# A scan layer and its router: dot products on TensorE, statistics spread, products in place

## The chip, the cores and the metric

The kernel runs on one core of a Trainium2 chip. The metric is the device time of one execution in microseconds; three executions of the kernel before gave 4455.1, 4456.08 and 4457.46 us, so the median is 4456.08 us. A core has five engines that run their own instruction streams and wait for each other by semaphores: TensorE (PE in the profile), VectorE (DVE), ScalarE (ACT), GpSimd (POOL) and SyncE (SP), which here starts all the DMAs of the part in question.

## What is computed

Two layers. The first is a selective state space layer on 16 batches of 1024 rows of 512 numbers, the second a layer that lets only some rows through attention and an MLP, chosen by a router's score. Cut to what matters:

```python
xh = _layernorm(x)                                 # 16 x 1024 x 512
xp = einsum('bld,ed->ble', xh, x_proj_w)           # 64 for the rank, 16 B, 16 C
delta = softplus(einsum('blr,dr->bld', xp[..., :64], dt_proj_w) + dt_proj_b)
h = exp(delta * A) * h + delta * B * xh            # step by step over the 1024 rows
y = (h * C).sum(n) + xh * D                        # 16 states n
x1 = x + y
hn = _layernorm(x1)
weights = (hn @ router_w)[..., 0] + router_b[0]    # one score a row
# top_k of the scores picks rows; those go through attention and an MLP
out = x1 + (result for chosen rows, hn for the others)
```

## The kernel before

`scan_phase` is the first part. It runs over 16 batches; a loop body holds two of them (lines 829 and following on VectorE). A batch has 16 chunks of 32 channels, and a chunk has 4 groups g of 4 states, so that a tile (c, g) is 128 partitions (4 states x 32 channels) by 1024 rows. For each tile:

- ScalarE makes the decay exp(delta A) into one of three PSUM places (`exp_decay`, line 671), and once a chunk copies delta times x there (`copy_dx`, 677).
- VectorE multiplies that by B into `inp` (`make_input`, 810). For the fourth group (`OWN`) of the chunks in `OWN_AT`, 1 to 13, GpSimd does it from SBUF (917).
- VectorE runs the recurrence, one scan instruction, into `hid[:, g]` (821). It waits for `ch_ready` of the same group one chunk earlier, that is until GpSimd has read the old states.
- GpSimd multiplies `hid` by C into `ch` (955).
- TensorE sums the states into `ps_y` (`sum_states`, 444, behind the skip term, 439), ScalarE copies `ps_y` to `ysb` (`copy_y`, 684), TensorE turns it and adds x (`turn_y`, 455 and 456), and ScalarE writes x1 back into `xr` (`copy_x1`, 691).

Every engine's program is written out in order by hand. Beside a chunk's tiles stands work for the batch before and the batch after, put at a pair (c, g) or (c, place) by tables at the top of the file: in chunks 0 to 2 ScalarE takes the second statistics of the batch before (`SUMS2`, 17 steps: 8 sums, a mean, 8 sums of squares), in chunks 3 and 4 it makes the output rows (`MAKE_OUT`), in chunks 5 and 6 the first statistics of the next batch (`SUMS1`), in 7 to 10 it normalises and copies the transposes made by TensorE (`TURN`, `COPY_XHAT`), in 10 and 11 the projections (`PROJECT`, `COPY_PROJ`, 404 and 545), and from 12 on delta (`Z`, `LOG`, 415, 563 to 581). GpSimd does ten steps of 128 x 1024 for delta (`DELTA`), small Newton series for both statistics (`FINISH1`, `FINISH2`, 878 to 887) and the end of the router (`route`, 906 and 909). `aux` is one PSUM bank which all these side jobs of TensorE pass through one after the other, in the order of `USES`.

The router before: ScalarE copies `router_w` into `aux` (`copy_rw`, 590), and VectorE takes eight dot products of 128 rows by 512 channels (`router`, 834), four after the scans of chunk 2 and four after those of chunk 3, each with the mean as its scalar. `make_out` overwrites the rows and waits for them. After the last batch the same work stands alone: `copy_rw`, the 17 steps, the router, Newton, `route`, a transpose of all the scores (505), and their DMA; behind that VectorE picks rows by the scores.

`ffn_phase`, with attention and MLP, follows at about 3475 us and is not touched.

## Time and profile before

| | |
|---|---|
| median of 3 executions | 4456.08 us |
| profiled execution | 4463.26 us |
| its span, first to last instruction | 4461.5 us |
| mean granted TensorE clock | 0.756 |
| VectorE busy | 3768.9 us (84%) |
| GpSimd busy | 3363.5 us (75%) |
| TensorE busy (matmul) | 3066.8 us (69%) |
| ScalarE busy | 2861.0 us (64%) |

The profile is of one execution. Busy shares are means over the whole span with its two phases. A timeline row gives the start in us from the span's start, the time of one instruction or of a run of equal ones (x4), the engine, the line, what is written and read, and in brackets the idle time before it and what ended it. Matmuls of float32 stand in the profile as two instructions each, with two weight loads.

### The profile page before, as it was taken

The numbers are of one execution on the slowest core, as the hardware profiler recorded it, in microseconds if no ns is written. First come the engines' busy times: TensorE is split into PE (matmuls) and PEld (weight loads), VectorE is DVE, ScalarE is ACT, GpSimd is POOL, SyncE is SP. The second block draws the span as 40 slices with busy tenths as digits, with TensorE's granted clock in tenths as the row PEclk, the third lists the DMA queues.
The fourth block names the chain that finished last, engine by engine and source line by source line (L and its number), as shares of the span: only waits on it lengthen the run. The fifth ranks groups of instructions, "written<-read, shape, count | busy, mean of one in ns | idle before, by whom it ended". The sixth has DMA issues, their size and how long they took to land. (4 is left out here: it accounts for less than half of the span.)

```text
span 4461.5 us, 61468 instructions
## 1 busy us (share of the span) xinstructions
PE 3066.8 (69%) x17574; PEld 1408.3 (32%) x17574; DVE 3768.9 (84%) x3027; ACT 2861.0 (64%) x4425; POOL 3363.5 (75%) x1716
## 2 busy tenths in 40 slices
PE   4667665766676666665665756666664289999997
PEld 1222232322232222222232323222222145555553
DVE  2999999999999999999999999999998754555552
ACT  5777777777778687868777777777774223332221
POOL 3999999999999999999999999999998100000010
PEclk7767676767766676667676767676775589999998
DMA  4454546463646455554545464636453300000000
GB/s 102 104 136 121 148 114 158 96 170 87 171 101 156 114 144 130 127 136 122 134 123 135 124 152 105 164 84 180 92 146 76 144 22 20 19 19 19 19 19 8
DMA packets 198219, 472.94 MB, mean 106 GB/s; under 512 B 60688, under 2 KB 61200, under 8 KB 197088
## 3 DMA queue, kind: packets, MB, share of 16 engines
q1 hardware_dynamic: 177136, 452.11, 40.3%
q0 software_dynamic: 20736, 16.88, 1.4%
q8 instruction: 135, 2.21, 0.2%
...
## 5 line engine op out<-in xcount | busy, mean ns | idle before, releaser
L955 POOL TENSOR_TENSOR ch<-hid,cmat 128x1024 f32<-128x1024 f32 x1024 | 2385.4, 2358 | 92.7 <-DVE hid L821 76.4
L821 DVE TENSOR_TENSOR_SCAN hid<-place,inp 128x1024 f32<-128x1024 f32 x1024 | 2266.1, 2270 | 105.4 <-ACT place L671 87.3
L671 ACT ACTIVATE place<-delr,a_neg 128x1024 f32<-128x1024 f32 x1024 | 1126.8, 1111 | 293.6 <-DVE hid L821 190.2
L444 PE MATMUL ps_y<-ch,nsum 128*32 128x256 f32 x8192 | 856.5, 517 | 424.3 <-POOL ch L955 423.4
L810 DVE TENSOR_TENSOR inp<-place,bmat 128x1024 f32<-128x1024 f32 x816 | 941.6, 1211 | 64.2 <-ACT place L677 63.4
L455 PE MATMUL ps_y<-ident,ysb 128*128 128x128 f32 x1024 | 319.2, 408 | 599.0 <-ACT ysb L684 580.0
L444 PEld LDWEIGHTS ps_y<-ch,nsum 128*32 128x32 f32 x8192 | 254.6, 137 | 1025.6 <-POOL ch L955 753.2
L917 POOL TENSOR_TENSOR inp<-dxr,bmat 128x1024 f32<-128x1024 f32 x208 | 490.2, 2357 | 0.0
L455 PEld LDWEIGHTS ps_y<-ident,ysb 128*128 128x128 f32 x1024 | 230.5, 278 | 807.9 <-ACT ysb L684 759.1
...
L439 PE MATMUL ps_y<-xhT,dskip 128*32 128x256 f32 x2048 | 260.8, 600 | 134.2 <-ACT xr L691 134.2
L677 ACT ACTIVATE place<-dxr 128x1024 f32<-128x1024 f32 x256 | 261.7, 1022 | 95.9 <-DVE hid L821 92.9
L456 PE MATMUL ps_y<-xr,ident 128*128 128x128 f32 x1024 | 286.6, 377 | 0.0
L456 PEld LDWEIGHTS ps_y<-xr,ident 128*128 128x128 f32 x1024 | 241.0, 289 | 0.0
L415 PE MATMUL aux<-xpT,dtw 64*128 64x512 f32 x256 | 218.2, 946 | 21.3 <-ACT dxT L564 20.5
L1282 PE MATMUL ps_t<-w,h2T 128*128 128x512 f32 x512 | 226.2, 600 | 0.7 <-ACT h2T L1423 0.7
L691 ACT ACTIVATE xr<-ps_y 128x256 f32<-128x256 f32 x256 | 97.6, 381 | 195.0 <-PE ps_y L456 194.3
L1306 PE MATMUL ps_m<-w,gT 128*128 128x512 f32 x512 | 222.4, 592 | 0.0
L1182 POOL COPY idx_x<-cols_i 128x1 uint32 (+1 forms) x16 | 3.0, 185 | 250.7 <-DMA out_rows<-row,idx_out 175.7
L609 ACT ACTIVATE squares<-xr,m 128x512 bf16<-128x512 f32 x256 | 181.2, 710 | 0.6
L1699 DVE COPY msel<-ps_m 128x128 f32<-128x128 f32 x16 | 4.7, 292 | 208.9 <-PE ps_m L1351 208.0
L684 ACT ACTIVATE ysb<-ps_y 128x256 f32<-128x256 f32 x256 | 94.0, 367 | 120.1 <-PE ps_y L444 120.1
...
## 6 DMA issues: line engine op xcount, KB each, us to landing
dxr<-dxT SPq DMA_DIRECT2D x1024, 128.0 KB, 2.4
delr<-delT SPq DMA_DIRECT2D x1024, 128.0 KB, 2.4
...
bmat<-b_and_c SPq DMA_DIRECT2D x256, 128.0 KB, 3.4
cmat<-b_and_c SPq DMA_DIRECT2D x256, 128.0 KB, 3.1
...
```

The lines of the kernel that those rows point to most:

```text
L439: pe.matmul(ps_y[q * CH:(q + 1) * CH, 0:2 * P], dskip[:, k, c % NT * CH:(c % NT + 1) * CH], xhT[:, i, j, q * 2 * P:(q + 1) * 2 * P], start ...
L444: last = pe.matmul(ps_y[q * CH:(q + 1) * CH, 0:2 * P], nsum[:], ch[:, g, q * 2 * P:(q + 1) * 2 * P], start=False, stop=(g == GROUPS - 1))
L455: pe.matmul(out_t, ysb[:, t * P:(t + 1) * P], ident[:], start=True, stop=False)
L456: last = pe.matmul(out_t.rearrange("p (q d) -> p q d", q=4), ident[:], x_t, start=False, stop=True)
L671: nc.scalar.activation(place[:, PLACE[par, c, g], :], delr[:, c % 2, :], ACT.Exp, scale=a_neg[:, i:i + 1])\
L677: nc.scalar.activation(place[:, PLACE[par, c, "dx"], :], dxr[:, c % 2, :], ACT.Copy).then_inc(dx_ready, 1)
L810: nc.vector.tensor_tensor(inp[:, g, :], place[:, PLACE[par, c, "dx"], :], bmat[:, g, :], ALU.mult).then_inc(inp_ready, 1)
L821: nc.vector.tensor_tensor_scan(hid[:, g, :], place[:, PLACE[par, c, g], :], inp[:, g, :], 0.0, ALU.mult, ALU.add).then_inc(hid_ready, 1)
L917: nc.gpsimd.tensor_tensor(inp[:, OWN, :], dxr[:, c % 2, :], bmat[:, OWN, :], ALU.mult)\
L955: nc.gpsimd.tensor_tensor(ch[:, g, :], hid[:, g, :], cmat[:, g, :], ALU.mult).then_inc(ch_ready, 1)
L1282: last = pe.matmul(one[bank], xT[:, k, :], w(k), start=(k == 0), stop=(k == n - 1))
L1306: last = pe.matmul(one["m1"], gT[:, k, :], w_2[:, k, :], start=(k == 0), stop=(k == F // P - 1))
```

## The change

Three things, all in `scan_phase`.

1. The router's scores come from TensorE. A row's dot product of x1 with `router_w` is split in two. The x part: `w_xproj` gets 32 more columns that all hold `router_w`, so that the projection of the normalised rows yields a further line block of `xpT`; `router_x` brings it into rows by 8 matmuls of one column, `copy_router_x` copies them, and `scale_route_x` on GpSimd undoes the normalisation (times the standard deviation, plus mean times the sum of `router_w`). The y part: `ysb` keeps all 16 chunks of a batch, and `router_y` multiplies each chunk (two blocks of 128 rows as weights) with 4 columns of `rw_chunk`, in five pieces (`ROUTE_Y`) during chunks 0 and 1 of the next batch. `copy_router_y` copies the result, and `route` on GpSimd puts the parts together, with 5 instructions in place of 2. VectorE's `router` and ScalarE's `copy_rw` go. The first `ADD_TERMS` entries move from chunks 0 and 1 to 1 to 3, and a delta step from chunk 2 to 3. For the last batch the five pieces stand at the end, in front of the statistics.
2. `SUMS1` begins at (5, 0) with one step for each place, and waits for each half of the rows by itself.
3. GpSimd writes its product with C over `hid`; `ch` goes. A scan now waits for `ch_summed`, TensorE's sum, of the same group one chunk earlier.

Besides, `OWN_AT` becomes chunks 2 to 12, so that VectorE makes two more input products a batch and GpSimd two fewer.

```diff
--- before.py
+++ after.py
-SUMS1 = {(5, 3): range(0, 3), (6, 0): range(3, 6), (6, 1): range(6, 9), (6, 2): range(9, 13), (6, 3): range(13, 17)}
+SUMS1 = {(5, 0): range(0, 1), (5, 1): range(1, 2), (5, 2): range(2, 3), (5, 3): range(3, 5), (6, 0): range(5, 7),
+         (6, 1): range(7, 10), (6, 2): range(10, 13), (6, 3): range(13, 17)}
...
-         (2, 3): (0, 2, 3), (7, 3): (0, 3, 3)}
-
-
-ADD_TERMS = {(2, 0): ((0, 2), (0, 3), (1, 1)), (2, 1): ((1, 1), (1, 2), (2, 1)),
+         (3, 1): (0, 2, 3), (7, 3): (0, 3, 3)}
...
-ADD_TERMS = {(2, 0): ((0, 2), (0, 3), (1, 1)), (2, 1): ((1, 1), (1, 2), (2, 1)),
+         (3, 1): (0, 2, 3), (7, 3): (0, 3, 3)}
+
+
+ADD_TERMS = {(2, 0): ((1, 3), (1, 3), (2, 1)), (2, 1): ((2, 1), (2, 2), (3, 0)),
...
-RW_COPY = (2, 1)
-ROUTER = (2, 3)
+ROUTE_Y = {(0, 1): range(0, 4), (0, 2): range(4, 6), (0, 3): range(6, 11), (1, 1): range(11, 14), (1, 2): range(14, 16)}
+COPY_ROUTE_Y = (2, 0)
+ROUTE_X = (14, 0)
+COPY_ROUTE_X = (14, 3)
+SCALE_ROUTE_X = (15, 1)
+ROUTE_READ = {cs[0]: i + 1 for i, cs in enumerate(ROUTE_Y.values())}
...
-OWN_AT = tuple(range(1, 14))
+OWN_AT = tuple(range(2, 13))
...
-        xproj = sb("xproj", [P, KD, R + 2 * N])
+        xproj = sb("xproj", [P, KD, P])
...
-        ch = sb("ch", [P, GROUPS, L])
-        ysb = sb("ysb", [P, 2 * P])
+        ysb = sb("ysb", [P, CHUNKS, 2 * P])
...
-                    last = pe.matmul(aux[0:R + 2 * N, :], xproj[:, k, :],
+                    last = pe.matmul(aux[:], xproj[:, k, :],
...
-                if k == 3 and h == 0 and has(b, 1):
-                    pe.wait_ge(router_sum, b * TC)
...
+            def router_x(b):
+
+                aux_free(b, ("route_x",))
+                for t in range(TC):
+                    last = pe.matmul(aux[:, t:t + 1], xpT[R + 2 * N:P, t * P:(t + 1) * P],
+                                     ident[R + 2 * N:P, R + 2 * N:R + 2 * N + 1], start=True, stop=True)
+                last.then_inc(aux_full, 1)
+
+            def router_y(b, cs, emptied):
+
+                if 0 in cs:
+                    pe.wait_ge(aux_emptied, emptied)
+                for c in cs:
+                    for t in range(2):
+                        last = pe.matmul(aux[:, 4 * t:4 * t + 4], ysb[:, c, t * P:(t + 1) * P], rw_chunk[:, c, :],
+                                         start=(c == 0 and t == 0), stop=(c == CHUNKS - 1 and t == 1))
+                last.then_inc(route_y_full, 1)
...
+                    if (k, h) == (2, 0) and has(b, 1):
+                        pe.wait_ge(route_y_copied, b)
...
-                                     ch[:, g, q * 2 * P:(q + 1) * 2 * P],
+                                     hid[:, g, q * 2 * P:(q + 1) * 2 * P],
...
+                        if (c, g) in ROUTE_Y and has(b, 1):
+                            router_y(b - 1, ROUTE_Y[c, g], b * NUSE + USE["z", 2, 1] + 1)
+                        if (c, g) == ROUTE_X and not final:
+                            router_x(b + 1)
...
+            for cs in ROUTE_Y.values():
+                router_y(nb_run - 1, cs, nb_run * NUSE)
...
-            def copy_rw(b, emptied):
-
-                act.wait_ge(aux_emptied, emptied)
-                nc.scalar.activation(aux[:], rw[:], ACT.Copy).then_inc(rw_ready, 1)
+            def copy_router_x(b):
+
+                if has(b, 1):
+                    act.wait_ge(route_in_step, b * 3)
+                aux_filled(b, ("route_x",))
+                nc.scalar.activation(route_x[:], aux[:, 0:TC], ACT.Copy).then_inc(aux_emptied, 1)
+
+            def copy_router_y(b):
+
+                if has(b, 1):
+                    act.wait_ge(wcol_ready, b)
+                act.wait_ge(route_y_full, b * len(ROUTE_Y) + len(ROUTE_Y))
+                nc.scalar.activation(route_y[:].rearrange("p (q t) -> p t q", t=2),
+                                     aux[:, 0:TC].rearrange("p (t q) -> p t q", t=2), ACT.Copy)\
+                    .then_inc(route_y_copied, 1)
...
+                for h in range(2):
+                    if 4 * h in steps:
+                        act.wait_ge(x_in[par][h], (b - par) * 8 + 16)
...
-                    act.wait_ge(ln2, b * LN2 + LN2 - 1)
-
-                    act.wait_ge(router_sum, b * TC + t + 4)
+                    act.wait_ge(ln2, b * LN2 + LN2)
...
-                nc.scalar.activation(ysb[:], ps_y[:, 0:2 * P], ACT.Copy).then_inc(ysb_ready, 1)
+                if c in ROUTE_READ and has(b, 1):
+                    act.wait_ge(route_y_full, (b - 1) * len(ROUTE_Y) + ROUTE_READ[c])
+                nc.scalar.activation(ysb[:, c, :], ps_y[:, 0:2 * P], ACT.Copy).then_inc(ysb_ready, 1)
...
-            copy_rw(last, nb_run * NUSE)
+            copy_router_y(last)
...
-                    dve.wait_ge(ch_ready, tile(b, c, g) - GROUPS + 1)
+                    dve.wait_ge(ch_summed, tile(b, c, g) - GROUPS + 1)
...
-            def router(b, par, h):
-
-                if h == 0:
-                    dve.wait_ge(rw_ready, b + 1)
-                    if has(b, 1):
-                        dve.wait_ge(wcol_ready, b)
-                    dve.wait_ge(ln2_act, b * LN_ACT + 9)
-                for t in range(4 * h, 4 * h + 4):
-                    if has(b, 1) or t > 0:
-                        dve.wait_ge(router_sum, b * TC + t)
-                    nc.vector.scalar_tensor_tensor(junk[:], xr[:, par, t, :], m2[:, 1, t:t + 1], aux[:],
-                                                   ALU.add, ALU.mult, accum_out=r2[:, 8, t:t + 1])\
-                        .then_inc(router_sum, 1)
...
-            last = nb_run - 1
-            for h in range(2):
-                router(last, 1, h)
...
+                nc.gpsimd.tensor_tensor(r1[:, 7, :], r1[:, 0, :], r1[:, 4, :], ALU.mult).then_inc(ln1, 1)
...
-            def route(b):
-
-                pool.wait_ge(router_sum, b * TC + TC)
-                nc.gpsimd.tensor_tensor(r2[:, 3, :], r2[:, 8, :], r2[:, 4, :], ALU.mult).then_inc(ln2, 1)
+            def scale_route_x(b, par):
+
+                n = b * 3
+                pool.wait_ge(aux_emptied, b * NUSE + USE["route_x",] + 1)
+                pool.wait_ge(ln1, b * LN1 + LN1)
+                if has(b, 2):
+                    pool.wait_ge(route_step, (b - 1) * ROUTE_STEPS)
+                nc.gpsimd.tensor_tensor(route_in[:, par, 1, :], m1[:, 1, :], rw_sum[:].to_broadcast([P, TC]), ALU.mult)\
+                    .then_inc(route_in_step, 1)
+                nc.gpsimd.tensor_tensor(route_in[:, par, 0, :], route_x[:], r1[:, 7, :], ALU.mult)\
+                    .then_inc(route_in_step, 1)
+                pool.wait_ge(route_in_step, n + 2)
+                nc.gpsimd.tensor_tensor(route_in[:, par, 0, :], route_in[:, par, 0, :], route_in[:, par, 1, :],
+                                        ALU.subtract).then_inc(route_in_step, 1)
+
+            def route(b, par):
+
+                n = b * ROUTE_STEPS
                 pool.wait_ge(ln2, b * LN2 + LN2)
+                pool.wait_ge(route_y_copied, b + 1)
+                pool.wait_ge(route_in_step, b * 3 + 3)
+                if has(b, 1):
+                    pool.wait_ge(wcol_ready, b)
+                nc.gpsimd.tensor_tensor(route_t[:, 0, :], m2[:, 1, :], rw_sum[:].to_broadcast([P, TC]), ALU.mult)\
+                    .then_inc(route_step, 1)
+                nc.gpsimd.tensor_tensor(route_t[:, 1, :], route_y[:], route_in[:, par, 0, :], ALU.add)\
+                    .then_inc(route_step, 1)
+                pool.wait_ge(route_step, n + 2)
+                nc.gpsimd.tensor_tensor(route_t[:, 2, :], route_t[:, 1, :], route_t[:, 0, :], ALU.add)\
+                    .then_inc(route_step, 1)
+                pool.wait_ge(route_step, n + 3)
+                nc.gpsimd.tensor_tensor(route_t[:, 1, :], route_t[:, 2, :], r2[:, 4, :], ALU.mult)\
+                    .then_inc(route_step, 1)
+                pool.wait_ge(route_step, n + 4)
                 pool.sem_inc(refining, 1)
-                nc.gpsimd.tensor_tensor(wcol[:, bass.ds(b * TC, TC)], r2[:, 3, :], rb[:].to_broadcast([P, TC]),
+                nc.gpsimd.tensor_tensor(wcol[:, bass.ds(b * TC, TC)], route_t[:, 1, :], rb[:].to_broadcast([P, TC]),
...
-                            pool.wait_ge(ch_summed, tile(b, c, g) - GROUPS + 1)
-                        nc.gpsimd.tensor_tensor(ch[:, g, :], hid[:, g, :], cmat[:, g, :],
+                        nc.gpsimd.tensor_tensor(hid[:, g, :], hid[:, g, :], cmat[:, g, :],
...
+                        if (c, g) == SCALE_ROUTE_X and not final:
+                            scale_route_x(b + 1, 1 - par)
...
-        "w_xproj": rows(i["L0_attn_x_proj_w"].T),
+        "w_xproj": rows(np.concatenate(
+            [i["L0_attn_x_proj_w"].T, np.repeat(i["L0_ffn_router_w"].reshape(D, 1), P - R - 2 * N, axis=1)], axis=1)),
...
+        "router_chunk": np.stack([np.concatenate([i["L0_ffn_router_w"].reshape(CHUNKS, CH).T if q == j
+                                                  else np.zeros((CH, CHUNKS), np.float32) for q in range(4)])
+                                  for j in range(4)], axis=2),
```

## Rows read from the trace of the kernel before

**Rows 1.** The page's busy tenths in 40 slices of the span, VectorE's line.

```profile
DVE  2999999999999999999999999999998754555552
```

**Rows 2.** What line 829 (the loop) left, in the view of one line.

```profile
L829 DVEq ALU_OP  x7: 40/40/40, 321.2 to 2857.2; - x7
```

**Rows 3.** Timeline, VectorE, batch 3: start us, us, engine, line, operation, out<-in, count, wait.

```profile
865.59 8.82 DVE L821 TENSOR_TENSOR_SCAN hid<-place,inp 128x1024 f32<-128x1024 f32 x4
...
877.71 8.82 DVE L821 TENSOR_TENSOR_SCAN hid<-place,inp 128x1024 f32<-128x1024 f32 x4
...
890.96 8.82 DVE L821 TENSOR_TENSOR_SCAN hid<-place,inp 128x1024 f32<-128x1024 f32 x4
```

**Rows 4.** Timeline, GpSimd, from chunk 12 of batch 3 to chunk 0 of batch 4.

```profile
867.95 9.30 POOL L955 TENSOR_TENSOR ch<-hid,cmat 128x1024 f32<-128x1024 f32 x4 [0.51 <-DVE hid L821]
...
880.07 2.34 POOL L955 TENSOR_TENSOR ch<-hid,cmat 128x1024 f32<-128x1024 f32 x1 [0.50 <-DVE hid L821]
...
921.68 11.63 POOL L955 TENSOR_TENSOR ch<-hid,cmat 128x1024 f32<-128x1024 f32 x5
```

**Rows 5.** Window of 211 us over batch 4: busy time of each engine, clock, DMA.

```profile
942.00:1153.00 211.00, 136.22 (x864) 59.19 (x856) 202.26 (x132) 160.85 (x246) 203.90 (x101) 0.72 0.52 126
```

**Rows 6.** What ended the idle time before line 821 (the scan).

```profile
  ACT place L671: 87.3, 59
```

**Rows 7.** Timeline, VectorE, chunk 1 of batch 4; in brackets the wait and its releaser.

```profile
931.25 2.29 DVE L821 TENSOR_TENSOR_SCAN hid<-place,inp 128x1024 f32<-128x1024 f32 x1 [1.20 <-ACT place L671]
...
937.94 4.47 DVE L821 TENSOR_TENSOR_SCAN hid<-place,inp 128x1024 f32<-128x1024 f32 x2 [1.20 <-POOL ch L955]
```

**Rows 8.** Timeline, ScalarE, chunk 0 of batch 4.

```profile
925.23 0.38 ACT L684 ACTIVATE ysb<-ps_y 128x256 f32<-128x256 f32 x1 [3.98 <-PE ps_y L444]
...
927.78 0.38 ACT L691 ACTIVATE xr<-ps_y 128x256 f32<-128x256 f32 x1 [1.25 <-PE ps_y L456]
```

**Rows 9.** Timeline, all engines, chunk 7 of batch 4.

```profile
1015.47 2.34 POOL L955 TENSOR_TENSOR ch<-hid,cmat 128x1024 f32<-128x1024 f32 x1 [0.51 <-DVE hid L821]
...
1019.44 4.47 DVE L821 TENSOR_TENSOR_SCAN hid<-place,inp 128x1024 f32<-128x1024 f32 x2 [1.87 <-ACT place L671]
...
1024.05 1.22 PE L444 MATMUL ps_y<-ch,nsum 128*32 128x256 f32 x16
```

**Rows 10.** Timeline, VectorE, the router's first four dot products, batch 3.

```profile
955.15 0.75 DVE L834 SCALAR_TENSOR_TENSOR junk<-xr,m,aux 128x512 bf16<-128x512 f32 x1 [0.62 <-ACT aux L590]
...
958.20 3.48 DVE L810 TENSOR_TENSOR inp<-place,bmat 128x1024 f32<-128x1024 f32 x3
```

**Rows 11.** Timeline, GpSimd, a series of five small instructions and what follows.

```profile
1018.32 0.20 POOL L878 TENSOR_TENSOR r<-r 128x8 f32<-128x8 f32 x1 [0.51 <-ACT r L643]
...
1019.72 7.00 POOL L955 TENSOR_TENSOR ch<-hid,cmat 128x1024 f32<-128x1024 f32 x3
```

**Rows 12.** Timeline, TensorE: turn_y at half clock, a sum, four passes of projection.

```profile
926.68 0.63 PE L455 MATMUL ps_y<-ident,ysb 128*128 128x128 f32 x2
927.11 0.63 PE L456 MATMUL ps_y<-xr,ident 128*128 128x128 f32 x2
...
1052.24 0.64 PE L444 MATMUL ps_y<-ch,nsum 128*32 128x256 f32 x8 [0.41 <-POOL ch L955]
...
1059.64 3.09 PE L404 MATMUL aux<-xhT,xproj 128*96 128x512 f32 x4
```

**Rows 13.** Timeline, ScalarE, chunk 10: the copy of a projection.

```profile
1065.31 0.59 ACT L545 ACTIVATE xpT<-aux 96x512 f32<-96x512 f32 x1 [3.88 <-PE aux L404]
```

**Rows 14.** End of the scan phase: timeline, then a window with the clock (0.50).

```profile
3450.58 0.38 ACT L691 ACTIVATE xr<-ps_y 128x256 f32<-128x256 f32 x1 [2.17 <-PE ps_y L456]
...
3451.38 0.62 ACT L603 ACTIVATE squares<-xr 128x512 bf16<-128x512 f32 x1
...
3463.02 0.08 DVE L834 DVE_READ_ACCUMULATOR junk<-xr,m,aux 128x1 f32 x1
...
3451.40:3465.00 13.60, 0.00 (x0) 0.00 (x0) 6.05 (x16) 11.64 (x37) 1.22 (x7) 0.50 0.43 155
```

62 lines of the change are left out of this document (39 added, 23 removed).

## Prediction

> **What bounds the kernel now.** I read the page first. The span of 4461.5 us has two parts: until about 3475 us the scan phase runs, in which VectorE is busy nine tenths or more in every slice, and behind it the attention and MLP phase, which the change doesn't touch [rows 1]. So only the scan phase matters. It handles 16 batches, and the loop over pairs of batches comes round every (2857.2 - 321.2)/6 = 422.7 us, that is 211.3 us a batch [rows 2]. Then I read the grouped instructions of the steady part, the timelines of VectorE, GpSimd and ScalarE over batch 4, and the end of the phase.
>
> VectorE: a chunk is four scans and three input products, one of the four products being GpSimd's: 877.71 - 865.59 = 12.12 us, or 890.96 - 877.71 = 13.25 us where VectorE makes all four. So one product costs VectorE 1.13 us and a scan 2.18 us [rows 3]. GpSimd: products at a pitch of 9.30/4 = 2.32 us; per batch 64 with C, 13 inputs and 10 steps for delta make 202 us, and small ones some 4 [rows 4]. A window of a batch's length has VectorE busy 202.3 and GpSimd 203.9 of 211 us [rows 5]: both are nearly full, so what matters is which of them waits, and where. VectorE's waits before a scan are almost all for the decay that ScalarE writes: 87.3 us in 59 pieces [rows 6].
>
> They stand in two places, which cut a batch into two stretches. **Stretch A** goes from the first scan of chunk 13 (877.71) to the third scan of the next batch's chunk 1 (937.94): 60.2 us. VectorE doesn't set it, it waits 1.20 us before the first scan of chunk 1, somewhat less before the second and 1.20 us before the third [rows 7]. (The profile names GpSimd's product for that last wait; but the one it needs, the fourth of the five of 921.68, was done at 931 [rows 4]. It is the decay.) GpSimd does: from 880.07 it runs 12 products and 7 delta steps without a gap until 924.0; 1.2 us later ScalarE copies ysb (925.23), 2.55 us later x1 (927.78), and a full ScalarE brings the decay after another 10.2 us [rows 4, 8]. 2.4 + 43.9 + 1.2 + 2.55 + 10.2 = 60.2: the chain closes. **Stretch B**, from there to the next chunk 13, is about 149.9 us here (211.3 less A; A is some 2.6 us longer in every second batch, where the loop jumps), and VectorE sets it: scans, products, the router's eight dot products, and one wait of 1.87 us in chunk 7 behind the statistics of the next rows [rows 9].
>
> **The change, part by part.**
>
> *Router off VectorE.* Its four dot products of chunk 2 take 958.20 - 955.15 = 3.05 us, behind a wait of 0.62 us that not every batch has [rows 10]; four more stand in chunk 3. That lies in stretch B, on the path: 2 x 3.05 and 0.2 for the waits, -6.3 us a batch.
>
> *Input products moved.* GpSimd keeps 11 instead of 13; chunk 1's and chunk 13's go to VectorE, 1.13 us each [rows 3]. Chunk 1's lies in front of the wait of 1.20 us in stretch A and costs nothing (the cover is ScalarE's lateness). Chunk 13's stands at the end of stretch B: +1.1 us. What GpSimd saves, 2 x 2.32 us, is worth nothing at chunk 13: it waits 0.50 us there for the scan today [rows 4]. At chunk 1 it lowers its backlog.
>
> *Scale of the first router part.* Three small GpSimd instructions after the second product of chunk 15. Small ones run at a pitch of 0.28 us [rows 11], so 0.85 us (bounds 0.6, three times the bare 0.20, and 1.4, a whole series of five). They stand in the middle of A's gapless GpSimd run: +0.85 us, and nothing covers them. On VectorE's side A then takes three chunks of 13.25, one more, two scans and a wait at the last scan of chunk 0, some 59.5 us, still under 61.1.
>
> *Output products in place, and the scan's new wait.* A scan now waits until TensorE has summed the product of the chunk before, not until GpSimd has read the states. Between the end of a scan and the start of the one that reuses its buffer lie 12.12 - 2.18 = 9.9 us. Needed are GpSimd's backlog, 2.34 us for the product, and the sum: 0.64 us at TensorE's full clock [rows 12], under twice that at half. So the wait begins when backlog and TensorE's lateness (its sum included) together pass 7.5 us. In chunks 0 and 15 GpSimd is furthest behind: product (15,3) ends at 924.0 + 0.85, its sum some 1.1 later, and the fourth scan of chunk 0 is delayed by 1 to 2 us; it lies in A, under ScalarE's chain.
>
> *GpSimd's backlog in B.* This is the term I had to choose. Of stretch B's relief GpSimd gets less: at 11.6 us a chunk against VectorE's 12.12 it gains 0.5 us a chunk, while a delta step moved from chunk 2 to 3, another in 7, two Newton series (1.7 each) and five route instructions (1.6 instead of 0.6) cost 9 us. Today the router's 6 us let it catch up. So it will be 3 to 5 us behind from chunk 4 to 10. Then TensorE's step sizes and transposes, which stand behind those sums, come later, and ScalarE, which waits for them in order, brings the decays later: the decay of (5,2) follows a step size, and those of chunk 11 a projection, for which it waits 3.88 us [rows 13] and which is hardly early then. Bounds: 0, if these slacks hold, and the whole 3 us of backlog. I take 0.9 us, as TensorE's lateness today comes mostly from ScalarE's copies and not from GpSimd, so that only part of a later product passes through.
>
> *Statistics spread.* The 17 steps keep their cost; the first ones move up into short idle times of ScalarE in chunk 5. If that idle time stayed, up to 1.9 us of chunk 7's wait would go; but the backlog fills it from the other side. I take -0.2 (bounds 0 and -1.9). The first half of the rows is asked for a chunk ahead of the second and so is there earlier; the second half is asked for no earlier than before.
>
> *TensorE's small matmuls.* Five pieces, 32 matmuls a batch of two passes each, with 128 x 128 weights and 4 columns, and 8 with one column. Two passes with 128 columns take 927.11 - 926.68 = 0.43 us at half clock [rows 12], so 0.215 each and 0.11 at full clock, an upper bound; half of that if only the weights count. In the loop that is 4 to 14 us a batch on an engine busy 136 of 211 us [rows 5]; the pieces stand right behind a sum, and the next comes 2.3 us later, so at most the piece of ten delays turn_y of chunk 0, by under 1 us, in front of slack. The Trainium skill (TensorE: Matmul & The Clock Gate, LDWEIGHTS) speaks against the form: a weight load is priced by its columns, P/1.2 ns, so 107 ns each however few columns are then multiplied. By that figure an estimate for 64 loads is 6.8 us, between my bounds; no row here shows such a matmul.
>
> *Tail.* After the last chunk all 32 come at once, and ScalarE's copy of their result stands ahead of the 17 statistics steps. Today those start 0.8 us after x1 (3450.58), and the router's eight run beside them and end at 3463.1, before the Newton series can [rows 14]. So removing them gives nothing here, and the 64 passes are all on the path: 3.5 us (full clock, weights only) to 13.8 us (half clock, all counted). The granted clock is 0.50 there [rows 14]; I take 6.3, between, as 4 columns are nearer to the weights alone, plus 0.7 for the longer route.
>
> *Head.* One more pass over router_w (0.7 us) ahead of the first statistics and one more constant: +1.5. ADD_TERMS later, wider projections and one more ln1 product are hidden or under 0.3 us.
>
> **Sum.** A: +0.85 x 15 = +12.8. B: (-6.3 + 1.1 + 0.9 - 0.2) = -4.5 x 14 = -63.0; last batch, without next rows, -5.2; first batch, which has no router, +1.0. Head +1.5, tail +7.0. Together -45.9 us. The profiled execution took 4463.3 us (span 4461.5), 7 more than the median of 4456.1; so 4417 for a profiled one and **4410 us** for the median.
>
> **Rivals.**
> - *The full gain.* The backlog costs nothing and chunk 7's wait goes: B -7.1, A as above or with the scale hidden, -6.3 to -7.1 a batch: 4456 - 95 + 8 = 4369, or 4382 with the scale. For it: the decays are 3 us early in most chunks. Against: GpSimd would have 203.0 us of work in 204 to 205, and must still wait at chunk 13. Chance 0.13.
> - *Eaten by ScalarE.* The backlog of 3 to 5 us passes through in full at chunks 3, 5, 9 and 11, another 2.5 to 3.5 us a batch: 4447 to 4460, the change worth nothing. For it: the chain GpSimd, TensorE, ScalarE, decay is tight at chunk 11 today already. Chance 0.15.
> - *Slower: the scan behind TensorE.* TensorE works in order, and sums come late where it stands behind turn_y, transposes and projections; the sum of (7,0) begins 6 us after its product's end today (ScalarE's copy is late), and in chunk 10 four passes of projection come first (3.09 us at half clock) [rows 9, 12]. If such lateness adds to the backlog instead of overlapping it, 7.5 us is passed in chunks 7, 8 and 10 and in 0 and 1 behind the new pieces: an estimate of 4.4 + 0.7 + 0.7 + 1.2 = 7 us a batch, net +2.5 to +3: about 4500. It decides when backlog plus lateness is over 7.5 us in more than two chunks of a batch. Chance 0.09.
> - *The change does less than it says* (in place products slower than 2.36 us, say): 0.1 us each would be 64 x 0.1 on GpSimd, half passed on; no reason seen, inside the range.
>
> **How the numbers follow.** Forecast case 0.63, with 4385 to 4440; full gain 0.13; eaten 0.15; slower 0.09. About 0.2% (9 us) is what a measurement can tell from no change. Faster: 0.63 + 0.13 + 0.05 (the better third of the eaten case) = 0.81; same 0.10; slower 0.09. The range of 8 in 10 takes the forecast's own bounds (tail +/- 6, scale +/- 6, backlog 0 to +1.5 a batch), half of the full gain and most of the eaten case: 4375 to 4448.
>
> **What would show it.** The loop should come round every 415 to 417 us. VectorE's busy time in the phase falls by about 16 x 6.1 less 32 x 1.2 us; GpSimd falls about 32 x 2.35 less 16 x 1.9. Stretch A should be 61.1 us with GpSimd's run 0.85 longer; VectorE should wait at the last scan of chunk 0 for TensorE, 1 to 2 us, and little for it elsewhere. B should be near 145. In the tail, the statistics should start some 6 us later after x1. Wrong would be: waits of scans for L444 in the middle chunks (the slower rival), waits for decays in chunks 3, 5, 9 or 11 of over 1 us (the eaten case), or a GpSimd that is never late.

## The result, and the profile after

The changed kernel took 4480.34 us (median of 7 runs, 4468.75 to 4487.48), the kernel before 4456.18 us (7 runs, 4452.09 to 4460.87) beside it. The ratio is 1.0048, 95% interval 1.0035 to 1.0061: half a per cent slower, where the forecast was 4410 us and the range ended at 4448. The profiled execution took 4481.62 us, span 4479.8; that of before had 4463.26 and 4461.5.

The page of after, where it answers the table and [rows 1, 2]:

```profile
span 4479.8 us, 62884 instructions
PE 3248.5 (73%) x18854; PEld 1606.1 (36%) x18854; DVE 3720.9 (83%) x2803; ACT 2845.9 (64%) x4443; POOL 3308.9 (74%) x1796
...
L1023 POOL TENSOR_TENSOR hid<-hid,cmat 128x1024 f32<-128x1024 f32 x1024 | 2387.5, 2360 | 116.1 <-DVE hid L880 102.9
L880 DVE TENSOR_TENSOR_SCAN hid<-place,inp 128x1024 f32<-128x1024 f32 x1024 | 2275.9, 2272 | 164.2 <-ACT place L722 131.1
```

The work did go where the change sends it: the router's instructions are gone from VectorE, GpSimd's product in place takes 2360 ns. Yet the scans now wait 164.2 us, where they waited 105.4 before. The waits, asked for the same stretch (400 to 3500 us) in both kernels, first three of before and then those of after (us in total, times, longest):

```profile
ACT xr L691 <- PE ps_y L456: 176.6, 190, 4.3
...
POOL r L878 <- ACT r L643: 27.4, 14, 16.1
...
DVE hid L821 <- ACT place L671: 75.5, 52, 3.0
```

```profile
ACT xr L744 <- PE ps_y L488: 262.7, 185, 4.7
...
POOL r L917 <- ACT r L696: 73.7, 21, 28.5
...
DVE hid L880 <- ACT place L722: 114.6, 106, 2.4
DVE hid L880 <- PE ps_y L476: 23.4, 28, 1.4
```

ScalarE waits 86 us more for turn_y, GpSimd 46 us more for the second statistics (12 of them in the tail, 28.5 for 16.1), VectorE 39 us more for decays and 23.4 us for TensorE's sums, which is the new wait.

To place that I worked out, from the starts of the scans in each trace, how long each chunk lasts: from its first scan to that of the next, mean over batches 1 to 14, in us. 12.12 is a chunk with three products on VectorE, 13.25 one with four [rows 3].

```text
chunk      0     1     2     3     4     5     6     7    8-11    12    13    14    15    batch
before   14.20 14.46 15.37 15.16 12.12 12.12 12.12 14.50 12.12 12.12 13.36 13.25 13.88  211.13
after    14.70 14.16 12.95 12.85 13.16 12.86 13.48 14.80 12.12 13.25 13.25 13.31 14.39  211.64
```

The router's 3 us have left chunks 2 and 3 each. Chunks 2 to 7 give 0.83 + 0.73 + 1.04 + 0.74 + 1.36 + 0.30 = 5.0 us back, chunk 12 the 1.13 us of the product moved to VectorE. Chunks 8 to 11 are untouched. Chunks 0, 1 and 13 to 15 add another 0.7. So a batch is 0.5 us longer where I had it 3.65 shorter. With the first batch (204.6 us before, 208.8 after) and the last (204.0, 201.7), and 1.9 us of the head, the phase grows by 14 x 0.5 + 4.2 - 2.3 + 1.9 = 10.8 us.

**Where the 5 us arise** is seen best in batch 5, in which both waits below are longer than in the mean (its chunks 2 to 7 begin at 1164.83, 1178.51, 1191.71, 1204.87, 1217.42, 1230.89). TensorE at the end of chunk 1 and in chunk 2:

```profile
1163.41 1.50 PE L444 MATMUL aux<-rw_chunk,ysb 128*128 128x4 f32 x12
1164.84 0.64 PE L476 MATMUL ps_y<-hid,nsum 128*32 128x256 f32 x8
1165.41 1.31 PE L444 MATMUL aux<-rw_chunk,ysb 128*128 128x4 f32 x8
...
1168.01 2.07 PE L458 MATMUL aux<-dxT,ident 128*128 128x512 f32 x2 [0.28 <-ACT route_y L639]
...
1173.09 1.02 PE L458 MATMUL aux<-delT,ident 128*128 128x512 f32 x2
1173.95 0.39 PE L487 MATMUL ps_y<-ident,ysb 128*128 128x128 f32 x2
```

The router's sum holds the bank `aux` until ScalarE copies it at (2,0), so the four terms of delta (2,0), which the new ADD_TERMS puts all at (1,3), come in one block of eight passes: 1173.95 - 1168.01 = 5.94 us at a granted clock of 0.59, all of it ahead of turn_y of chunk 1. In the kernel before the same eight passes stand at (0,2) and (0,3), with a sum between, and TensorE waits 2.5 us for ysb behind them:

```profile
932.09 1.19 PE L426 MATMUL aux<-dxT,ident 128*128 128x512 f32 x2
...
935.60 1.02 PE L426 MATMUL aux<-delT,ident 128*128 128x512 f32 x2
939.15 0.80 PE L455 MATMUL ps_y<-ident,ysb 128*128 128x128 f32 x2 [2.53 <-ACT ysb L684]
```

In after ScalarE has copied ysb at 1169.73 and pays for the block, in front of the last of the second statistics (first row: 4.03 us here, 2.92 in the mean of batches 1 to 14, where before has 0.13):

```profile
1175.04 0.38 ACT L744 ACTIVATE xr<-ps_y 128x256 f32<-128x256 f32 x1 [4.03 <-PE ps_y L488]
...
1180.36 0.21 ACT L696 ACTIVATE r<-r 128x8 f32<-128x8 f32 x1
...
1197.36 0.38 ACT L737 ACTIVATE ysb<-ps_y 128x256 f32<-128x256 f32 x1 [2.22 <-PE ps_y L476]
...
1201.33 0.38 ACT L744 ACTIVATE xr<-ps_y 128x256 f32<-128x256 f32 x1 [2.67 <-PE ps_y L488]
```

GpSimd, in order, meets the Newton series of these statistics (FINISH2, at (2,3)) before they are there, and then the five route instructions of chunk 4:

```profile
1180.64 0.20 POOL L917 TENSOR_TENSOR r<-r 128x8 f32<-128x8 f32 x1 [4.16 <-ACT r L696]
...
1205.36 0.20 POOL L967 TENSOR_TENSOR route_t<-m,rw_sum 128x8 f32<-128x8 f32 x1
...
1206.70 2.35 POOL L1023 TENSOR_TENSOR hid<-hid,cmat 128x1024 f32<-128x1024 f32 x1
```

It stands 4.16 us for nothing (2.95 us in the mean, 1.5 to 4.4). From there its products begin 3 to 6 us behind the ends of their scans through chunks 3 to 5 (before: 0.1 to 1.1 us in batch 5), TensorE's sums come late, ScalarE's copies wait 2.2 and 2.7 us for them (the block before this one), and VectorE finds decays missing (rows of chunks 3, 3, 5, 6 and 7; a wait in front of a chunk's first scan counts in the length of the chunk before):

```profile
1178.51 2.29 DVE L880 TENSOR_TENSOR_SCAN hid<-place,inp 128x1024 f32<-128x1024 f32 x1 [1.47 <-ACT place L722]
...
1181.76 6.65 DVE L880 TENSOR_TENSOR_SCAN hid<-place,inp 128x1024 f32<-128x1024 f32 x3 [0.97 <-ACT place L722]
...
1204.87 4.47 DVE L880 TENSOR_TENSOR_SCAN hid<-place,inp 128x1024 f32<-128x1024 f32 x2 [0.70 <-ACT place L722]
...
1223.13 4.47 DVE L880 TENSOR_TENSOR_SCAN hid<-place,inp 128x1024 f32<-128x1024 f32 x2 [1.20 <-ACT place L722]
...
1238.60 2.29 DVE L880 TENSOR_TENSOR_SCAN hid<-place,inp 128x1024 f32<-128x1024 f32 x1 [2.39 <-ACT place L722]
```

**The end of the phase**, answering [rows 14], first ScalarE and TensorE behind the last chunk, then the window with its clock (columns: stretch, length, busy time of PE, PEld, DVE, ACT, POOL, granted clock, DMA share, GB/s):

```profile
3460.66 13.65 PE L444 MATMUL aux<-rw_chunk,ysb 128*128 128x4 f32 x64
3460.91 0.38 ACT L744 ACTIVATE xr<-ps_y 128x256 f32<-128x256 f32 x1 [1.70 <-PE ps_y L488]
3474.42 0.18 ACT L639 ACTIVATE route_y<-aux 128x8 f32<-128x8 f32 x1 [13.12 <-PE aux L444]
...
3460.66:3474.30 13.64, 13.64 (x65) 13.57 (x64) 0.00 (x0) 0.38 (x1) 0.00 (x0) 0.50 0.43 154
```

The statistics begin 13.7 us after x1 instead of 0.8. Cut at two rows, the end of the last scan and the start of GpSimd's last route instruction, the executions compare so (us):

```text
                      last scan ends   to the route   from there to the end
before                    3444.46          20.86            996.18
after                     3455.26          34.11            990.43
e_tail                    3455.85          20.93            990.02
e_inplace                 3441.63          21.31            990.86
e_norouter                3452.71          20.63            990.36
```

The scan phase (with the head) is 10.8 us longer and the tail 13.25 us; together 24.1, which is what the medians differ by (24.2). The last column shows that some 5 us of what before's profiled execution had over its median lay behind the scans.

### The profile page after: what moved, and what is told of

Read it like the earlier page. It is cut to its first block and busy times, and to the rows that moved or that the text cites. A ratio compares the mean times of both kernels' runs of the same rounds, so it can differ in the third digit from the quotient of the medians.

```text
span 4479.8 us, 62884 instructions
## 1 busy us (share of the span) xinstructions
PE 3248.5 (73%) x18854; PEld 1606.1 (36%) x18854; DVE 3720.9 (83%) x2803; ACT 2845.9 (64%) x4443; POOL 3308.9 (74%) x1796
## 5 line engine op out<-in xcount | busy, mean ns | idle before, releaser
L1023 POOL TENSOR_TENSOR hid<-hid,cmat 128x1024 f32<-128x1024 f32 x1024 | 2387.5, 2360 | 116.1 <-DVE hid L880 102.9
L880 DVE TENSOR_TENSOR_SCAN hid<-place,inp 128x1024 f32<-128x1024 f32 x1024 | 2275.9, 2272 | 164.2 <-ACT place L722 131.1
L476 PE MATMUL ps_y<-hid,nsum 128*32 128x256 f32 x8192 | 846.3, 509 | 470.1 <-POOL hid L1023 464.8
L869 DVE TENSOR_TENSOR inp<-place,bmat 128x1024 f32<-128x1024 f32 x848 | 976.7, 1210 | 64.5 <-ACT place L728 64.1
L476 PEld LDWEIGHTS ps_y<-hid,nsum 128*32 128x32 f32 x8192 | 241.8, 133 | 1022.5 <-POOL hid L1023 782.8
L487 PE MATMUL ps_y<-ident,ysb 128*128 128x128 f32 x1024 | 301.2, 389 | 390.2 <-ACT ysb L737 372.0
L487 PEld LDWEIGHTS ps_y<-ident,ysb 128*128 128x128 f32 x1024 | 220.3, 264 | 574.4 <-ACT ysb L737 504.5
L987 POOL TENSOR_TENSOR inp<-dxr,bmat 128x1024 f32<-128x1024 f32 x176 | 414.9, 2357 | 0.0
L488 PE MATMUL ps_y<-xr,ident 128*128 128x128 f32 x1024 | 275.3, 364 | 0.0
L488 PEld LDWEIGHTS ps_y<-xr,ident 128*128 128x128 f32 x1024 | 228.7, 275 | 0.0
L427 PE MATMUL aux<-xpT,dtw 64*128 64x512 f32 x256 | 194.4, 848 | 20.0 <-ACT dxT L604 18.4
```

The costliest lines, as they stand in the source:

```text
L476: last = pe.matmul(ps_y[q * CH:(q + 1) * CH, 0:2 * P], nsum[:], hid[:, g, q * 2 * P:(q + 1) * 2 * P], start=False, stop=(g == GROUPS - 1))
L487: pe.matmul(out_t, ysb[:, c, t * P:(t + 1) * P], ident[:], start=True, stop=False)
L488: last = pe.matmul(out_t.rearrange("p (q d) -> p q d", q=4), ident[:], x_t, start=False, stop=True)
L869: nc.vector.tensor_tensor(inp[:, g, :], place[:, PLACE[par, c, "dx"], :], bmat[:, g, :], ALU.mult).then_inc(inp_ready, 1)
L880: nc.vector.tensor_tensor_scan(hid[:, g, :], place[:, PLACE[par, c, g], :], inp[:, g, :], 0.0, ALU.mult, ALU.add).then_inc(hid_ready, 1)
L987: nc.gpsimd.tensor_tensor(inp[:, OWN, :], dxr[:, c % 2, :], bmat[:, OWN, :], ALU.mult)\
```

## Experiments

Ratios are to the kernel before, run beside on the same chip; a difference to after is that of the two ratios, times 4456 us. A ratio is known to about 0.1%, so such a difference is uncertain by some 7 us. Chunk lengths are means as above, from the one profiled execution, which can lie off its kernel's median: 6.6 us below in e_newton, 6.2 below in e_terms, 7 above in e_few, 8.9 above in e_relief. My theory was that the loss comes from TensorE's new work and what it shifts (the block of terms, late statistics, GpSimd's wait, the backlog). Against it stood first the scan behind TensorE through the product in place, and at last that the router's time on VectorE had served the other engines to catch up, so that its removal is eaten by whatever means it is done. The letters in the expectations are explained in each; P is the theory of placement, first explained in e_inplace, T the theory that TensorE has no room in chunks 1 and 2 whatever the order.

**e_inplace**: the kernel before with the product in place and the scan's wait on the sum, nothing else.

```diff
-                                     ch[:, g, q * 2 * P:(q + 1) * 2 * P],
+                                     hid[:, g, q * 2 * P:(q + 1) * 2 * P],
...
-                    dve.wait_ge(ch_ready, tile(b, c, g) - GROUPS + 1)
+                    dve.wait_ge(ch_summed, tile(b, c, g) - GROUPS + 1)
...
-                        nc.gpsimd.tensor_tensor(ch[:, g, :], hid[:, g, :], cmat[:, g, :],
+                        nc.gpsimd.tensor_tensor(hid[:, g, :], hid[:, g, :], cmat[:, g, :],
...
```

> The kernel before with one part of the change alone: GpSimd writes its product over hid, and a scan waits for TensorE's sum of the chunk before. Theory P (placement: what the change lost lies in chunks 1 to 3, in side work that was put in front of turn_y and in a Newton series that GpSimd has to wait for) expects no difference, 4452 to 4462 us, with VectorE waiting about 1 us at the fourth scan of chunk 0 in every second batch, under cover of ScalarE. Theory S (the scan's wait on TensorE is what costs) expects 0.7 to 2 us a batch, 4466 to 4490 us. Theory G (GpSimd has too little room anywhere, so every added microsecond of its work or wait costs) expects no difference.

4457.16 us, ratio 1.0004 (0.9994 to 1.0013); all chunks within 0.14 us of before, the batch 211.01. The edit costs nothing, as P expected, and the slower rival falls with it.

**e_norouter**: that, with the new OWN_AT and the new SUMS1 (the spread first statistics, waiting for each half of the rows by itself); the router stays on VectorE.

```diff
-OWN_AT = tuple(range(1, 14))
+OWN_AT = tuple(range(2, 13))
...
```

> The kernel before with all of the change but the router: products in place, two more input products a batch on VectorE, statistics spread. The router's dot products stay on VectorE. P and G expect +1.1 us a batch for chunk 13's product and 0 to -0.7 for the spread statistics: 4462 to 4475 us, with chunks 2 to 6 as long as before (12.12 us in 4 to 6), because the router's 6 us still let GpSimd catch up. S expects 4476 to 4500.

4465.67 us, 1.0023 (1.0013 to 1.0033), within the range of P. Chunk 12 becomes 13.25 (+1.13, as in the sum), chunk 7 falls from 14.50 to 13.60, chunks 4 to 6 stay at 12.12. So all parts but the router make +10 us, and moving the router to TensorE adds 11 us more, though it takes 6.3 us a batch off VectorE. All of the loss in chunks 4 to 6 comes with moving the router.

**e_newton**: after, with the second statistics' Newton series one place later.

```diff
-FINISH2 = (2, 3)
+FINISH2 = (3, 0)
```

> The changed kernel with GpSimd's second Newton series one tile later, FINISH2 at (3, 0) in place of (2, 3). P expects GpSimd's wait of some 4 us for ScalarE in front of the series gone, its backlog in chunks 3 to 6 down from over 5 to 1 to 2 us, and 2 to 3 us a batch of the waits in chunks 4 to 6 with it: 4435 to 4452 us. G expects the same, since it gives GpSimd time back. S expects no difference, 4470 to 4485.

4462.66 us, 1.0013 (1.0003 to 1.0022), 16 us less than after. Chunk 4 falls from 13.16 to 12.13 and chunk 5 from 12.86 to 12.30; chunk 6 stays at 13.43. In batch 5 the four scans of chunk 4 (first row) stand without a wait and those of chunk 5 (second row) with 0.2 us, where after has 0.70 and 0.31 us in chunk 5; the third row is chunk 6:

```profile
1182.36 8.82 DVE L880 TENSOR_TENSOR_SCAN hid<-place,inp 128x1024 f32<-128x1024 f32 x4
...
1194.48 9.01 DVE L880 TENSOR_TENSOR_SCAN hid<-place,inp 128x1024 f32<-128x1024 f32 x4
...
1212.49 4.47 DVE L880 TENSOR_TENSOR_SCAN hid<-place,inp 128x1024 f32<-128x1024 f32 x2 [1.20 <-ACT place L722]
```

GpSimd's wait for the statistics is all but gone, so it is a cause: 1.6 us a batch between these two profiled executions, 1.1 by the medians (16 us in 15 batches). The expected range was missed by 11 us at its upper end: more is lost elsewhere.

**e_pieces**: after, with the router's matmuls all in chunk 0, its copy at (1,1), and the first terms right behind.

```diff
-ADD_TERMS = {(2, 0): ((1, 3), (1, 3), (2, 1)), ...
+ADD_TERMS = {(2, 0): ((1, 1), (1, 2), (2, 1)), ...
...
-ROUTE_Y = {(0, 1): range(0, 4), (0, 2): range(4, 6), (0, 3): range(6, 11), (1, 1): range(11, 14), (1, 2): range(14, 16)}
-COPY_ROUTE_Y = (2, 0)
+ROUTE_Y = {(0, 0): range(0, 4), (0, 1): range(4, 8), (0, 2): range(8, 12), (0, 3): range(12, 16)}
+COPY_ROUTE_Y = (1, 1)
```

> The changed kernel with the router's small matmuls in four pieces, all in chunk 0 (after the sums of the four groups), their copy at (1, 1), and the first ADD_TERMS in two halves at (1, 1) and (1, 2) in place of both at (1, 3). P expects ScalarE's wait of 4 us for turn_y of chunk 1 to fall to 1 to 2, the second statistics to end 2 to 3 us earlier, GpSimd's wait for them to shrink by as much, and the waits of chunks 3 to 6 to fall: 4440 to 4458 us. S and G expect no change beyond 5 us, as the same passes of TensorE and the same GpSimd work are there: 4472 to 4485.

4514.43 us, 1.0135 (1.0118 to 1.0152): a clear miss of all three ranges. Chunk 3 does fall to 12.12, but chunk 1 rises from 14.16 to 18.15. In chunks 0 and 1 the sums are the latest anyway, and what is put between them is paid for at once. TensorE's idle time there, from the traces by chunk, is 3.6 us in chunk 1 and 7.3 in chunk 2 before, 0.7 and 1.1 after: there was no room for both the router's matmuls and the terms in chunks 0 and 1. That gave rise to T.

**e_terms**: after, with the terms one or two places later and spread, and the delta step behind them.

```diff
-         (3, 1): (0, 2, 3), (7, 3): (0, 3, 3)}
+         (3, 3): (0, 2, 3), (7, 3): (0, 3, 3)}
...
-ADD_TERMS = {(2, 0): ((1, 3), (1, 3), (2, 1)), (2, 1): ((2, 1), (2, 2), (3, 0)),
+ADD_TERMS = {(2, 0): ((2, 0), (2, 1), (2, 3)), (2, 1): ((2, 3), (3, 0), (3, 2)),
```

> The changed kernel with the terms of delta moved: ADD_TERMS (2, 0) in two halves at (2, 0) and (2, 1), copy at (2, 3), ADD_TERMS (2, 1) at (2, 3) and (3, 0), copy at (3, 2), and the delta step behind them at (3, 3). The first eight passes no longer stand between the sum of (1, 3) and turn_y of chunk 1, where they take 6 us at half clock. P (these passes in front of turn_y, and the Newton series that GpSimd meets too early) expects ScalarE's wait of 4 us for turn_y of chunk 1 to go, chunk 3 down by 0.7 us to 12.1, the statistics done some 3 us earlier, GpSimd's wait for them down to 1 or 2 us and with it 1 us or more of chunks 4 and 5: 4440 to 4460 us. G (GpSimd has too little room anywhere) expects 4470 to 4485, since its work stays. T (TensorE itself is full in chunks 1 and 2, whatever the order) expects the waits to appear in chunk 2 or 3 instead, as they did in chunk 1 when the terms were put there: 4475 or more.

4462.30 us, 1.0011 (1.0002 to 1.002). Chunks 2 to 5 fall to 12.25, 12.56, 12.87 and 12.23 from 12.95, 12.85, 13.16 and 12.86. ScalarE's wait for turn_y of chunk 1 falls to 1.26 us in the mean (2.92 in after), GpSimd's for the statistics to 0.86 (2.95). So the block ahead of turn_y is a cause as well, in part in the same chunks. The 16 us belong to the whole edit, which also moves the second terms and a delta step; P's range ends 2 us lower, T's begins 13 us higher.

**e_few**: after, with 5 of 16 chunks in the router's sum; it leaves out eleven sixteenths of the router's product with y.

```diff
-                for c in cs:
+                for c in (0,) if cs[0] == 0 else (cs[-1],):
```

> The changed kernel with only 5 of the 16 chunks in the router's small matmuls, one for each piece: 11 of 16 are left out, so that the scores and with them the chosen rows are not the reference's. It prices these matmuls. P expects nothing in the loop (the sum of (1, 3) waits for GpSimd, not for the piece before it) and 5 us less in the tail, where all stand alone: 4468 to 4478 us. T expects TensorE's room in chunks 1 and 2 to matter: 1 to 2 us a batch and the tail, 4445 to 4460.

4458.77 us, 1.0001 (0.9992 to 1.001). The tail takes 25.2 us to the route instead of 34.1, 8.9 us less. A batch is 211.11, 0.5 us less than after; but this profiled execution lies 7 us above its median, and by the medians 12 of the 21 us are left for the batches, 0.8 each. P had expected nothing in the loop and 4468 us or more: the time lies in the range written for T. So leaving out eleven of sixteen small matmuls is worth some 0.5 to 0.8 us a batch where they stand, and 8.9 us in the tail.

**e_tail**: after, with the last copy of the router's sum behind the last statistics.

```diff
-            copy_router_y(last)
             ln2_sums(last, 1, range(17))
+            copy_router_y(last)
```

> The changed kernel with ScalarE's copy of the router's y part behind the 17 statistics steps of the last batch, in place of in front of them, so that TensorE's 32 small matmuls run beside the statistics. All theories expect the tail's 7 us back and nothing else: between the last x1 and the first statistics step under 1 us, 4470 to 4477 us.

4466.73 us, 1.0019 (1.001 to 1.0028), 13 less than after, a little more than expected; the table above has the tail back at 20.93 us. What is left to wait for is 1.25 us:

```profile
3461.31 13.65 PE L444 MATMUL aux<-rw_chunk,ysb 128*128 128x4 f32 x64
...
3475.06 0.18 ACT L639 ACTIVATE route_y<-aux 128x8 f32<-128x8 f32 x1 [1.25 <-PE aux L444]
```

**e_combo**: after, with the edits of e_terms, e_newton and e_tail together.

> The changed kernel with three placements at once: the terms of delta as in e_terms, the Newton series at (3, 0), and the last copy behind the statistics. P expects the backlog of GpSimd in chunks 3 to 6 under 2 us, chunks 2 to 5 at 12.1 to 12.3 us, a loop of 416 to 418 us for two batches and 7 us less in the tail: 4415 to 4435 us, faster than both kernels. G expects 4445 to 4460. T expects 4455 or more.

4440.28 us, 0.9956 (0.9943 to 0.997), 41 us less than after and 20 less than before, between the ranges of P and of the others. Apart, the three gains add up to 45. A batch is 209.49 us, so the loop comes round every 419.0 us where P had 416 to 418. Chunks 2 and 3 keep 0.3 and 0.2 us over 12.12, chunks 4 and 5 0.6 and 0.3, chunk 6 all of its 1.4.

**e_routed**: e_combo with the five route instructions moved from GpSimd's backlog in chunk 4 to chunk 10.

```diff
-ROUTED = (4, 2)
+ROUTED = (10, 2)
```

> e_combo with one thing more: the five router instructions on GpSimd stand at (10, 2) in place of (4, 2), out of the stretch in which GpSimd is 3 to 5 us behind. G (what is left over 12.12 us in chunks 3 to 6, 2.5 us a batch, is GpSimd's backlog passing through TensorE and ScalarE to the decays) expects 1.3 us less backlog in chunks 4 to 6 and 0.4 to 0.9 us a batch less: 4426 to 4435 us. A (ScalarE's own work fills these chunks, whatever GpSimd does) expects 4437 to 4444.

4446.97 us, 0.9982 (0.9972 to 0.9991), a batch 209.74. Neither theory had it: no gain, and by the ratios a loss of 12 us, though the two profiled executions differ by 2.5 only. The backlog did fall: GpSimd's products begin 2.1 us behind their scans in chunk 5 and 0.7 in chunk 6, in e_combo 3.6 and 2.2. Chunk 5 is 12.54 all the same, 12.40 in e_combo. Why the shorter backlog brings nothing is open.

**e_relief**: e_routed with chunk 4's input product on VectorE, which takes 2.36 us off GpSimd there for 1.13 us.

```diff
-OWN_AT = tuple(range(2, 13))
+OWN_AT = (2, 3, 5, 6, 7, 8, 9, 10, 11, 12)
```

> e_routed with one more input product, that of chunk 4, moved from GpSimd to VectorE: 2.32 us a batch less backlog from chunk 4 on for 1.13 us more on VectorE. G expects chunks 4 to 6 together 1.5 to 2 us shorter than in e_combo, which about pays for the 1.13: 4422 to 4435 us. A expects 17 us more than e_routed: 4450 to 4460.

4439.25 us, 0.9952 (0.9935 to 0.9969), above G's range and below A's, from 4 runs that lie between 4426 and 4448. Chunks 4 and 5 are at 12.12, but chunk 3 takes 13.74 (12.43 in e_routed), and a batch 210.50. VectorE's added product gives ScalarE 1.1 us as well, so this doesn't separate GpSimd's backlog from ScalarE's own lateness as the cause in chunks 4 and 5. Chunk 6 still takes 13.45, with GpSimd's products 0.2 us or less behind there, so its loss is not the backlog:

```profile
1185.80 8.82 DVE L880 TENSOR_TENSOR_SCAN hid<-place,inp 128x1024 f32<-128x1024 f32 x4
...
1197.91 8.82 DVE L880 TENSOR_TENSOR_SCAN hid<-place,inp 128x1024 f32<-128x1024 f32 x4
...
1216.59 4.47 DVE L880 TENSOR_TENSOR_SCAN hid<-place,inp 128x1024 f32<-128x1024 f32 x2 [2.10 <-ACT place L722]
```

What ScalarE does before that decay shows one more wait, for the load of the next batch's rows. It stands in 13 of the batches 1 to 14, 0.70 us in the mean:

```profile
1212.84 0.63 ACT L654 ACTIVATE squares<-xr 128x512 bf16<-128x512 f32 x1 [1.53 <-DMA xr<-in_x]
```

**e_sums**: e_routed with the first statistics placed as before the change, and waiting for both halves of the rows before the first step.

```diff
-SUMS1 = {(5, 0): range(0, 1), (5, 1): range(1, 2), (5, 2): range(2, 3), (5, 3): range(3, 5), ...
+SUMS1 = {(5, 3): range(0, 3), (6, 0): range(3, 6), (6, 1): range(6, 9), (6, 2): range(9, 13), (6, 3): range(13, 17)}
...
-                for h in range(2):
-                    if 4 * h in steps:
+                if 0 in steps:
+                    for h in range(2):
                         act.wait_ge(x_in[par][h], (b - par) * 8 + 16)
...
```

> e_routed with the first statistics where the kernel before has them, from (5, 3) on. If the spread steps are what makes the decay of (6, 2) late, as they put 7 steps in front of it in place of 6, chunk 6 loses its 1.4 us and chunk 7 gains at most 0.9: 4420 to 4435 us. If the backlog is the cause, chunk 6 stays over 13 us and chunk 7 grows: 4435 to 4448.

4477.79 us, 1.0051 (1.0033 to 1.0068): both expected ranges are missed by far, 31 us over e_routed. Chunk 6 rises to 15.23 and chunk 7 to 15.10. The waits from 400 to 3500 us name the reason (total, times, longest):

```profile
ACT squares L653 <- DMA xr<-in_x: 30.6, 13, 3.7
```

The second half of the next rows lands 14.5 us into chunk 5, and the old statistics, put at the end of chunk 5, wait for it before their first step; in the mean of batches 1 to 14 ScalarE waits 2.4 us, in e_routed 0.3. The load lands at about 14 us in e_terms, e_combo, e_routed and e_relief too, at 9.9 in after and 9.0 before. So the spread steps are worth 31 us where the load comes that late. No run has the old steps with after's other placements, where it comes earlier.

**e_free**: the kernel before, each of the router's dot products over 8 of 512 channels; the other channels are left out.

```diff
-                    nc.vector.scalar_tensor_tensor(junk[:], xr[:, par, t, :], m2[:, 1, t:t + 1], aux[:],
+                    nc.vector.scalar_tensor_tensor(junk[:, 0:8], xr[:, par, t, 0:8], m2[:, 1, t:t + 1], aux[:, 0:8],
```

> The kernel before with the router's eight dot products over 8 of the 512 channels, and nothing else changed: the rest of each dot product is left out, so that the scores and the chosen rows are not the reference's. It measures the disputed term by itself: VectorE gets some 4.5 to 5 us a batch back, and no engine gets anything new to do. If VectorE alone sets chunks 2 to 6 (the prediction's term of -6.3 us), the time falls by 4.5 to 5 us in each of 15 batches: 4380 to 4392 us. If the router's time is also the time in which ScalarE and GpSimd catch up (theory C), waits for decays and for sums take part of it back, in chunks 3, 6 and 7 above all: 4395 to 4430.

4405.65 us against 4459.95 on that chip, 0.9885 (0.9868 to 0.9901). Its chunks:

```text
chunk      0     1     2     3     4     5     6     7    8-12    13    14    15    batch
e_free   14.05 14.46 13.24 13.09 12.12 12.12 12.31 14.68 12.12 13.39 13.25 13.94  207.24
```

A small dot product still takes 0.27 us, 942.31, 942.55, 942.82, 943.08 in batch 4, so four leave 1.0 us in each chunk. 4.2 us a batch were taken from chunks 2 and 3, and 3.9 of them remain in the batch; chunks 6 and 7 take 0.37 back, chunks 4 and 5 nothing. Fifteen times 3.9 is 58 us, the medians differ by 54. The time lies in the range written for C, but by the chunks C is worth a tenth of the gain. Two thirds of the router's 6.3 us, taken off VectorE, are worth nearly their full length if nothing else is moved for it; the last third was not tried.

## Why the prediction was wrong, and where it was right

**Stretch A** was right: 60.8 us (60.2 before, 61.1 forecast), the three scale instructions costing 0.6 us, the lower bound, as GpSimd's run grew from 43.95 to 44.55. VectorE's wait of 1.1 us for TensorE at the last scan of chunk 0 came in 9 of 15 batches, under ScalarE's chain and free (e_inplace has it too and costs nothing). The in-place product, the 1.13 us of chunk 13's product (between the first scans of 12 and 13) and the head (+1.9 for 1.5) were right as well. The first batch was not: +4.2 us for the 1.0 and the 0.85 of A. Chunk 1's product costs its full 1.12 us there (chunk 0 takes 17.74 us for 16.62), as no wait of ScalarE's covers it, and chunks 3 and 6 lose 0.8 and 0.9.

**Stretch B** was wrong: 149.7 us in the mean, as long as before, against a forecast of 145. The term of -4.5 us a batch measured nothing, and with it 63 of the 70 us between the forecast and the time. The router's 6.3 us did leave. The step that failed is the half sentence "ADD_TERMS later ... hidden or under 0.3 us", together with "the pieces stand right behind a sum, and the next comes 2.3 us later". I had counted the new passes against a TensorE that is busy 136 of 211 us of a batch, and looked at each piece alone. What counts is the order in two chunks: the bank that the router's sum holds pushes eight older passes, 5.94 us, in front of turn_y of chunk 1, where they had stood before a 2.5 us gap. e_terms shows that it is a cause (-16 us with what else it moves), e_pieces that chunk 1 has no room for a second placing. The new matmuls themselves, which I had put at nothing in the loop, take a part too: leaving out eleven of sixteen gave 0.5 to 0.8 us a batch (e_few).

**The backlog term** of 0.9 us was the second failure, and a consequence. The backlog itself was near the 3 to 5 us forecast; what I had not asked is what else makes GpSimd late. It meets FINISH2 4.16 us early, a wait that the prediction's inventory of moved steps lacked: the statistics were not moved, but what they wait for was. From there the "eaten by ScalarE" rival describes much of the loss. It named chunks 3, 5, 9 and 11, and decays do come late in front of the scans of 3 and 5, which shows in the lengths of chunks 2 to 5; 4 and 5 lose 1.8 us a batch, of which e_newton takes 1.6 away. 9 and 11 stay at 12.12, since GpSimd has caught up by 8. How the lateness passes from GpSimd to the decays is argued from rows; e_newton leaves GpSimd 3.4 and 3.8 us behind in chunks 4 and 5 (4.9 and 4.0 in after) and still has almost no loss there, and e_routed's shorter backlog gains nothing. The rival went to 4460 at most; the time passed it, because of the block in TensorE's queue, chunk 6 and the tail, which it did not contain.

**Chunk 6** (+1.36) isn't the backlog (e_relief). The traces show what it is: how early ScalarE is. The table has, in us and as means over batches 1 to 14, how long before the end of the preceding scan the decay of the second and of the third scan of chunk 6 is ready (negative: VectorE waits), and ScalarE's wait for the load of the next rows.

```text
                second   third   wait for the load   statistics
before           3.24     0.70         0.00           old
e_free           2.81     0.23         0.03           old
e_sums           2.16    -2.82         2.37           old
e_norouter       2.01     0.70         0.00           spread
after            0.25    -1.01         0.00           spread
e_relief         1.04    -1.03         0.70           spread
e_combo          0.51    -1.07         0.26           spread
```

Between the two decays ScalarE works on the statistics of the next rows: that costs 1.3 us of its lead with the spread steps and 2.6 with the old ones, and the wait for the load comes on top, in every line. So in after the lead is used up before chunk 6 (0.25 us are left of 2.0 in e_norouter), and in e_relief more than half of the loss is the load. What takes ScalarE's lead is in part what delays it in chunks 1 to 4: it starts the last output row of the batch before 11.2 us into chunk 4 in after, 9.8 in e_combo, 8.7 in e_relief, but 7.4 before and in e_norouter. Why so much stays lost in e_combo, and why the load lands later there, no run separates.

**The second rival**, slower by the scan behind TensorE, gave the right sign for a wrong reason: e_inplace costs nothing, and chunks 7, 8 and 10 show no such wait. That the kernel came out slower, as it alone said, is no merit of its. In the full-gain rival a sum was off: its 4369 already holds the scale, which 4382 adds again; that changes nothing here.

**Tail.** Predicted +7, measured 13.25; this term was mis-sized. The bounds were 3.5 to 13.8 and I took a value near the lower, "as 4 columns are nearer to the weights alone". All 64 passes take 13.65 us, 0.213 each, at a granted clock of 0.50: the two-pass 128-column row at that clock [rows 12] was no upper bound but the price. e_tail shows that it need not be paid at all: the copy had only to stand behind the statistics. The Trainium skill (TensorE: Matmul & The Clock Gate, LDWEIGHTS) prices a load by its 128 columns, at 107 ns. The passes at a granted clock of 1.00 come near that with 0.12 us; at 0.50 they take double, and there the measurement decides.

**Statistics spread**: -0.2 assumed, -0.9 a batch in chunk 7 shown with the router in place, and 31 us in all shown in e_sums, where the old steps run into the late load. An edit that seems to be worth little beside one placement may be worth much beside another.

What beats both kernels is the change with three of its places moved, e_combo at 0.9956, and with two more, e_relief at 0.9952, not to be told apart. They gain 20 us, where e_free gained 54 by taking 4.2 of the router's 6.3 us a batch off VectorE and moving nothing; and e_combo stays 30 us short of the forecast.
